# Exponentials of two units and of one in turn in six PSUM banks, and a burst of the other matmuls every three units

## The reference

```
c_kv = h @ W_dkv + b_dkv;  c_q = h @ W_dq + b_dq                      # width 128
k, v, q_base, q_rot from c_kv and c_q; k_rot = h @ W_kr; rotary on q_rot, k_rot
scores = einsum('bqhd,bkhd->bhqk', q, k) / sqrt(64)                   # 16 heads, 64 wide
out = softmax(scores) @ v
x = layernorm(h + out @ W_o + b_o)
x = layernorm(x + x @ int4_rounded(W_ffn) + b_ffn + (x @ a) @ b)
```

## Time and profile before

| | us |
|---|---|
| median of 3 runs | 2159.52 (2157.9 to 2245.24) |
| the profiled execution | 2158.53 |
| its slowest core's span (core 6) | 2157.0 |
| spans of the 8 cores | 2140.2 to 2157.0 |
| TensorE, ScalarE, VectorE busy | 1938.3, 2016.5, 602.7 |
| first and last start of an exponential | 121.2, 2088.5 |

### The profile page before, as it was taken

The page is one execution under the profiler, slowest core; times in us unless marked ns, Lnnn a source line. Parts: engine busy times, 40 slices in busy tenths (PEclk is TensorE's granted clock), DMA queues, the critical chain, the costliest instruction groups (busy, mean ns, idle before and its releaser), DMA issues.

```text
span 2157.0 us, 61016 instructions; the slowest of 8 cores (2140.2 to 2157.0 us)
## 1 busy us (share of the span) xinstructions
PE 1938.3 (90%) x22544; PEld 708.4 (33%) x22544; DVE 602.7 (28%) x1084; ACT 2016.5 (93%) x2177; POOL 256.6 (12%) x303
## 2 busy tenths in 40 slices
PE   5977888989999999998999999999999999999976
PEld 2422333333333333333333333333333333333323
DVE  2731411232223322222222322323222322322224
ACT  2689999989999999998999999999999999999973
POOL 2000000110011110110111100211111100211021
PEclk9999999999999999999999999999999999999998
DMA  9772300121122211221121211312121311323121
GB/s 166 164 148 80 107 23 27 51 92 43 36 83 67 87 45 53 71 71 69 41 93 50 99 36 36 103 54 81 45 92 48 102 31 41 102 85 118 41 70 39
DMA packets 78681, 155.69 MB, mean 72 GB/s; under 512 B 16192, under 2 KB 46912, under 8 KB 78400
## 3 DMA queue, kind: packets, MB, share of 16 engines
q1 hardware_dynamic: 64672, 106.86, 15.5%
q0 software_dynamic: 13728, 44.93, 8.7%
HBM read 109.75 MB, written 40.76 MB: 70 GB/s over the span
## 4 chain that ended last, share of the span: by engine, by line
ACT 69%; issue 16%; PE 6%; DMA 3%; DVE 2%; ACTq 2%; SPq 1%; POOL 0%; DVEq 0%; POOLq 0%
ACT Psb L1004 69%; ACTq L998 2%; DMA wbuf<-hG 1%; DMA rbc<-rec 1%; SPq L495 1%; PE PS L742 1%; PE PS L916 1%; PE PS L858 1%; PE PS L944 1%; DMA osb<-hG 1%; PE PS L729 1%; PE PS L879 1%; PE PS L774 1%; PE PS L769 1%; PE PS L754 1%
## 5 line engine op out<-in xcount | busy, mean ns | idle before, releaser
L1004 ACT ACTIVATE Psb<-PS 128x1024 bf16<-128x1024 f32 x2048 | 1933.9, 1025 | 34.8 <-PE PS L858 22.5
L858 PE MATMUL PS<-Qsb,Ksb 64*128 64x512 bf16 x4096 | 804.0, 387 | 149.4 <-ACT Psb L1004 138.5
L879 PE MATMUL PS<-Psb,Vsb 128*32 128x512 bf16 x8192 | 634.1, 386 | 0.5 <-ACT Psb L1004 0.5
L858 PEld LDWEIGHTS PS<-Qsb,Ksb 64*128 64x128 bf16 x4096 | 212.9, 93 | 702.5 <-issue 696.4
L889 PE MATMUL PS<-Psb,ones_sb 128*32 128x256 bf16 x8192 | 404.1, 274 | 3.5 <-issue 3.5
L889 PEld LDWEIGHTS PS<-Psb,ones_sb 128*32 128x32 bf16 x8192 | 221.7, 97 | 224.2 <-issue 8.1
L1154 DVE TENSOR_TENSOR X<-PS,X 128x512 f32<-128x512 f32 x112 | 77.5, 692 | 625.5 <-PE PS L835 330.0
L879 PEld LDWEIGHTS PS<-Psb,Vsb 128*32 128x32 bf16 x8192 | 127.9, 94 | 236.5 <-issue 236.5
L831 PE MATMUL PS<-wbuf,osb 128*128 128x512 bf16 x448 | 135.6, 384 | 0.0
L802 PE MATMUL PS<-wbuf,osb 128*128 128x512 bf16 x448 | 135.6, 384 | 0.0
L1126 DVE COPY rec<-PS 128x256 f32<-128x256 f32 x64 | 27.1, 423 | 344.9 <-PE PS L889 344.9
(11 more groups left out here) (111 smaller groups left out, 690.8 us busy)
## 6 DMA issues: line engine op xcount, KB each, us to landing
wbuf<-wo_p POOLq DMA_DIRECT2D x32, 512.0 KB, 7.0
rbc<-rec SPq DMA_DIRECT2D x512, 32.0 KB, 1.8
X<-h SPq DMA_DIRECT2D x28, 512.0 KB, 3.9
x_scr<-X SPq DMA_DIRECT2D x28, 512.0 KB, 2.6
X<-x_scr SPq DMA_DIRECT2D x28, 512.0 KB, 3.4
wbuf<-wf_p POOLq DMA_DIRECT2D x28, 512.0 KB, 6.9
out<-X SPq DMA_DIRECT2D x28, 512.0 KB, 2.6
X<-W_ffn SPq DMA_DIRECT2D x16, 512.0 KB, 4.4
```

The source lines that it names most:

```text
L858: m = pe.matmul(PS[:, b0 + 512 * hh:b0 + 512 * (hh + 1)], Ksb[rows, k0:k0 + 128], Qsb[rows, 512 * p:512 * (p + 1)], tile_position=(64 * hh ...
L879: pe.matmul(PS[32 * j:32 * (j + 1), b0:b0 + 512], Vsb[:, v0:v0 + 32], Psb[:, p0 + 512 * (j // 2):p0 + 512 * (j // 2 + 1)], start=first and ...
L1004: act.activation(Psb[:, 1024 * (g % 4):1024 * (g % 4 + 1)], PS[:, 1024 * (g % 2):1024 * (g % 2 + 1)], AF.Exp, scale=0.125).then_inc(sem["e ...
```

## The change

Three units now make one **period** (n in the code, 683 of them). Scores have six banks: the first two units of a period go to banks 0 to 3 and get one exponential of 2048 columns, the third goes to banks 4 and 5 and gets one of 1024. Values have bank 6 alone, and VectorE copies them to a new buffer xs at the end of a pair (pv_free lets the next pair's values in). Bank 7 is shared: in each period the side step writes it, VectorE empties it (side_out), the sums of the period write it, and VectorE adds them to rec (sums_in). On TensorE a period is: scores of the next period, then a burst of side step, values and sums. The o and f steps have 256 columns at 32-wide tiles, four at once, and each has half of the contraction, so there are 448 of them, each emptied by VectorE. One side step goes in a period; a planner (the while loop) gives 574 of the 683 periods one. The normalising steps are placed 1 to 5 periods after the pair's end: reciprocals 1, 2, 2, 3, DMAs 3, multiply 5. Exponential buffers in Psb are six units instead of four. The tail is the same but for the padded low-rank weights.

```diff
-    rec = sbt("rec", [128, 256], F32)
+    rec = sbt("rec", [128, 512], F32)
     rbc = sbt("rbc", [128, 512], F32)
+    xs = sbt("xs", [128, 512], F32)
...
+    NPER = (NG + 2) // 3
+    def per_units(n):
+        return range(3 * n, min(3 * n + 3, NG))
+    def parts(n):
+        us = per_units(n)
+        return [(P, [u for u in us if u // NKC == P])
+                for P in range(us[0] // NKC, us[-1] // NKC + 1)]
+    def end_of(P):
+        return ((P + 1) * NKC - 1) // 3
...
+    while main or qs:
+        whole = len(parts(n)) == 1
+        st = None
+        if qs and n >= want(qs[0]):
+            st = qs.pop(0)
+        elif main and n >= ready(main[0]) and (
+                whole or main[0][0] == "z" or main[0][1] == LAST - 1):
+            st = main.pop(0)
+        elif qs and n >= ready(qs[0]):
+            st = qs.pop(0)
+        if st:
+            when[st] = n
+            side[n] = st
+        n += 1
...
-        for k, off in enumerate((1, 2, 3, 4, 5, 5, 5 + max(1, NKC // 4 - 1))):
-            ep_at.setdefault(min((P + 1) * NKC + off, NG), []).append((P, k))
+        for k, off in enumerate((1, 2, 2, 3, 3, 5)):
+            ep_at.setdefault(min(end_of(P) + off, NPER), []).append((P, k))
...
+            def side_step(st, n):
+                qt, b0 = st[1], 3584
+                if n:
+                    pe.wait_ge(sem["den_free"], den_no[n - 1, parts(n - 1)[-1][0]] + 1)
...
+                if st[0] in ("o", "f"):
+                    sub, q, i = st[2:]
+                    f = st[0] == "f"
...
+                        w0 = 1024 * c + 256 * q
+                        for j in range(4):
+                            m = pe.matmul(PS[32 * j:32 * (j + 1), b0:b0 + 256],
+                                          osb_tok(qt, sub, c)[:, 32 * j:32 * (j + 1)],
+                                          wbuf[:, w0:w0 + 256], start=(c == 4 * i),
+                                          stop=(c == 4 * i + 3 and not (f and i)))
+                    if f and i:
+                        for j in range(4):
+                            m = pe.matmul(PS[32 * j:32 * (j + 1), b0:b0 + 256],
+                                          zb_sb[:, 32 * j:32 * (j + 1)],
+                                          bpad_sb[:, 256 * q:256 * (q + 1)], start=False, stop=True)
...
-                b0 = 1024 * (g % 2)
+                b0 = 1024 * (g % 3)
...
                     pe.wait_ge(ld_krot[kc // 4 % 2], 32 * (kc // 8 + 1))
-                if g >= 2:
-                    pe.wait_ge(sem["exp_done"], g - 1)
+                if g >= 3 and g % 3 != 1:
+                    pe.wait_ge(sem["exp_done"], g - 1 if g % 3 == 0 else g - 2)
...
+            def values(P, us):
+                p = P % NP
+                for u in us:
+                    if u == P * NKC:
+                        if P:
+                            pe.wait_ge(sem["pv_free"], P)
+                        else:
+                            pe.wait_ge(sem["ev_v"], 8 * NSP)
+                    p0 = 1024 * (u % 6)
                     for j in range(4):
                         v0 = 1024 * (u % NKC) + 128 * p + 32 * j
-                        pe.matmul(PS[32 * j:32 * (j + 1), b0:b0 + 512], Vsb[:, v0:v0 + 32],
-                                  Psb[:, p0 + 512 * (j // 2):p0 + 512 * (j // 2 + 1)],
-                                  start=first and u == g, stop=last and u > g)
-                if g == 0:
+                        m = pe.matmul(PS[32 * j:32 * (j + 1), 3072:3584], Vsb[:, v0:v0 + 32],
+                                      Psb[:, p0 + 512 * (j // 2):p0 + 512 * (j // 2 + 1)],
+                                      start=(u % NKC == 0), stop=(u % NKC == NKC - 1))
+                if us[-1] % NKC == NKC - 1:
+                    m.then_inc(sem["pv_end"], 1)
+            def sums(n, P, us):
+                if n == 0:
                     pe.wait_ge(sem["init"], 4)
-                if first and P:
-                    pe.wait_ge(sem["den_free"], P)
-                for u in (g, g + 1):
+                if den_no[n, P]:
+                    pe.wait_ge(sem["den_free"], den_no[n, P])
+                pe.wait_ge(sem["ev_misc"], misc_by[n])
+                for u in us:
                     for j in range(4):
-                        p0 = 1024 * (u % 4) + 256 * j
-                        m = pe.matmul(PS[32 * j:32 * (j + 1), 3072:3328], ones_sb[:, :],
-                                      Psb[:, p0:p0 + 256], start=first and u == g,
-                                      stop=last and u > g)
-                m.then_inc(sem["pv_done"], 2)
-            for g in range(NG):
-                scores(g)
-                if g % 2 and g >= 3:
-                    values(g - 3)
-                for st in bg_at.get(g, ()):
-                    if st[0] in ("qr", "qp"):
-                        q_step(st)
-                    else:
-                        tail_step(st)
-            values(NG - 2)
+                        p0 = 1024 * (u % 6) + 256 * j
+                        m = pe.matmul(PS[32 * j:32 * (j + 1), 3584:3840], ones_sb[:, :],
+                                      Psb[:, p0:p0 + 256], start=(u == us[0]), stop=(u == us[-1]))
+                m.then_inc(sem["den_done"], 1)
+            def burst(n):
+                pe.wait_ge(sem["exp_done"], per_units(n)[-1] + 1)
+                if n in side:
+                    side_step(side[n], n)
+                for P, us in parts(n):
+                    values(P, us)
+                    sums(n, P, us)
+            for u in per_units(0):
+                scores(u)
+            for n in range(NPER):
+                if n + 1 < NPER:
+                    for u in per_units(n + 1):
+                        scores(u)
+                burst(n)
             pe.wait_ge(sem["exp_done"], NG)
...
-                    act.wait_ge(sem["ev_v"], 8 * NSP)
-                act.activation(Psb[:, 1024 * (g % 4):1024 * (g % 4 + 1)],
-                               PS[:, 1024 * (g % 2):1024 * (g % 2 + 1)],
-                               AF.Exp, scale=0.125).then_inc(sem["exp_done"], 1)
+                if n == 1:
+                    act.wait_ge(sem["st_rqa"], 16)
+                    act.wait_ge(sem["st_rqc"], 16)
+                act.wait_ge(sem["s_done"], us[1] + 1)
+                p0 = 1024 * (us[0] % 6)
+                act.activation(Psb[:, p0:p0 + 2048], PS[:, 0:2048], AF.Exp, scale=0.125
+                               ).then_inc(sem["exp_done"], 2)
+                if len(us) == 3:
+                    if n == 0:
+                        act.wait_ge(sem["ev_v"], 8 * NSP)
+                    act.wait_ge(sem["s_done"], us[2] + 1)
+                    p0 = 1024 * (us[2] % 6)
...
+            def sums_in(n, P, us):
+                d = den_no[n, P]
+                acc, src = rec[:, 256 * (P % 2):256 * (P % 2 + 1)], PS[:, 3584:3840]
+                dve.wait_ge(sem["den_done"], d + 1)
+                if us[0] == P * NKC:
+                    if P >= 2:
+                        dve.wait_ge(sem["ld_rec"], 128 * (P - 1))
+                    if P == 0:
+                        dve.wait_ge(st_rk[1], 32 * (NSP // 2))
+                    dve.tensor_copy(acc, src).then_inc(sem["den_free"], 1)
+                else:
+                    dve.wait_ge(sem["den_free"], d)
+                    dve.tensor_tensor(acc, src, acc, op=ALU.add).then_inc(sem["den_free"], 1)
...
+            def values_out(P):
+                dve.wait_ge(sem["pv_end"], P + 1)
+                if P:
+                    dve.wait_ge(sem["nrm_done"], P)
+                else:
+                    dve.wait_ge(sem["rope_q"], 5)
+                dve.tensor_copy(xs[:, :], bank(6)).then_inc(sem["pv_free"], 1)
...
+                        dve.wait_ge(sem["mm_misc"], misc_no["f", qt - 2, 3, 3, 1] + 1)
+                    if p >= 3 and qt < LAST:
+                        if p == 4:
+                            dve.wait_ge(sem["st_rqc"], 16 * (qt + 2))
+                        elif p == 5:
+                            dve.wait_ge(sem["st_rqa"], 16 * (qt + 2))
+                        else:
+                            dve.wait_ge(sem["rope_q"], 5 * (qt + 2))
+                    dve.wait_ge(sem["pv_free"], P + 1)
+                    dve.tensor_tensor(osb_pair(qt, p), xs[:, :], rbc[:, :], op=ALU.mult
                                       ).then_inc(sem["nrm_done"], 1)
...
+                if st[0] == "z":
+                    dve.tensor_copy(zb_sb[:, :], PS[:, 3584:3712]).then_inc(sem["ev_misc"], 1)
+                if st[0] in ("o", "f"):
+                    sub, q, i = st[2:]
+                    n = ln_no(qt, 1 if st[0] == "o" else 2, sub)
+                    dve.wait_ge(sem["bias_in"], n + 1)
+                    dve.wait_ge(sem["ev_misc"], m)
+                    dve.tensor_tensor(Xq(n, q), PS[:, 3584:3840], Xq(n, q), op=ALU.add).then_inc(sem["ev_misc"], 1)
+                    if i and q % 2:
...
+            for n in range(NPER + 1):
+                if n < NPER:
```

(7 more changed lines are left out.)

488 lines of the change are left out of this document (231 added, 257 removed).

## The result

The changed kernel takes **2358.36 us** (median of 4 runs, 2356.32 to 2360.54), the kernel before beside it 2159.52 us: a ratio of 1.0918, 95% interval 1.0897 to 1.0939. In some executions of any kernel the cores of one die show a lower clock and take longer (one of the four of the kernel before took 2245.24 us); times and ratios in this document leave out those over 1% longer, and of the kernel "side step first", whose profiled execution has it mildly on cores 4 to 7, the periods are those of cores 0 to 3. The change is slower by 9%, inside the range and at its upper end: the profiled executions are 200 us apart (2358.62 against 2158.53), 143 were forecast.

A forecast was written before the change was run, and what follows sets the result against it. ScalarE's exponentials bound the kernel before, with TensorE close behind; VectorE's emptying would join the pacing loop. Terms 22+6-8+52+43+7+12+7+2 = +143 on 2158.5 gave 2300 us, range 2195 to 2360.

The forecast's parts named there:

- The loop (+22): Middle-tile periods with a side step: sums wait for VectorE to empty bank 7, 2.89 us against 2.853, +22 us.
- the first tile's +7: First tile: 85 periods at 2.75 instead of 2.79 us, plus six pair ends at 1.6 us, +7 us together.
- The multiply (+52): Normalising multiply five periods after a pair's end: VectorE waits for rec copies, delaying the next evacuation; 47 x 1.1, +52 us.
- Pair ends (+43): Periods where a pair ends: evacuation, xs copy and old sums delay the new pair's sums and scores; 36 x 1.2, +43 us.
- Double exponentials: ScalarE's 2048-column exponential: lasts 1.89 us at 0.87 per further 1024 columns; 1.86 to 1.92 would confirm the slope.
- The removed instruction: ScalarE: each of 683 removed exponentials saves 0.03 us, 20 us in all, only where it doesn't wait for scores.
- the clock: Rival: TensorE's granted clock falls to 0.97, each TensorE term longer, +30 us on the forecast, 2330 us; chance 0.10, mostly this.
- The rival in which VectorE's loop does not bind: Side step's sums start within 1.10 us, so the 2.75 loop or ScalarE's 2.67 holds: 2100 us; chance 0.09.
- A: The double exponential of a period on ScalarE, taken to last 1.89 us.
- The one in which its blocks do not bind: Rival: VectorE's loop binds, but copies land in time or pair ends fall into slack: 2190 us, about same; chance 0.17.

The follow-up runs named there:

- side step first: The changed kernel with the side step moved ahead of the third unit's scores and the wait for the period's exponentials: 2336.72 us, ratio 1.0796 to the kernel before.
- the short copy: The changed kernel with VectorE copying only 64 of the 512 values columns to xs at a pair's end: 2359.92 us, ratio 1.0922 to the kernel before.
- the run with two singles: The changed kernel with each double exponential split in two, each releasing its own scores: 2362.09 us, ratio 1.0890 to the kernel before.

## Why the prediction held, and where its sizes were off

**The loop (+22)** was right in kind and link by link, 0.08 long in 3; its size was small, since o and f periods away from the blocks have a mean of 2.97 where the loop had 2.89. It is told by the 443 waits, by the periods of the side step that fell when VectorE's emptying was cut, and by 2.79 when TensorE's order was turned. Periods without a side step have a median of 2.73, forecast 2.75. With +143 forecast and 149 us measured in periods at full clock, the sum of these terms stood, and not only by errors that cancel. By kind of period, over the 2.85 of before: end+6 with a side step 58 us (forecast 52), pair ends 40 (43), all others 54 (48). Inside the others two things do cancel: the first tile's +7 came out as nothing (2.82 us a period in both kernels), and the periods of the 28 transposing steps, for which the working has no term, measure 3.25, +10.

**The multiply (+52)** was the largest term and right in mechanism: right place (the burst at end+6), waits for rbc in every case, though of 2.3 us in 64 places and not of about 1 in 50. Taking it out is worth 69 us by ratio: (3.85 - 2.93) x 55 = 51 at its place, as forecast, of which other periods take 9 back ((3.070 - 3.008) x 682 = 42 in all at full clock), and 20 less in low-clock periods, for which the term had no place.

**Pair ends (+43)**: 3.93 against about 3.0 of the other periods of this kernel, 0.93 x 36 = 33 by the count of the forecast, which had 1.2 x 36 = 43. The working put xs on the path between the emptying and the old pair's sums; the short copy shows that the three uses of bank 7 alone give the same 3.9.

**Double exponentials**: 1.877 us, forecast 1.86 to 1.92. Slope from 1.018 for 1024: 0.859 for 1024 more, 0.16 fixed. The removed instruction was put at 0.03 us, from two-pointer rows; the run with two singles gives 1.96 - 1.88 = 0.08. The Trainium skill (ScalarE: Activation LUTs, What ACT_TABLE_LOAD costs) gives 186 ns and 0.833 ns a column, of which 93 ns overlap back to back; by that rule, an estimate, 1024 columns take 1.04 us, 2048 columns 1.89 and an instruction more costs 0.09, and the trace agrees within 0.01 to 0.02 us. It still changed nothing, as ScalarE does not set this pace.

**The missed terms.** First, the weights' maximum: its wait for two DMAs had 20.0 us in the trace of before, on VectorE, and I did not ask what the change queues behind it. About +15. Second, the clock: as a rival it had a chance of 0.10 and +30 on top of the forecast, 2330, and 0.97 at some 80% busy; measured are 0.97 at 82% and some +30 in low-clock periods beside the stall, so the forecast's mechanism and this rival came together, and 2358 lies nearer to 2330 than to 2300. These two are 45 of the 57 us between the terms' sum and the measured loss; 6 more are in the full-clock periods and 4 in the later start. That the result still lies inside the range, 2 us below its upper end, is in part luck: that end was made of the clock, 15 us at the multiplies and 50 us for a slower double exponential, which did not come, and nothing in it stood for the stall of the weights' maximum. The rival in which VectorE's loop does not bind fell: 139.9 us of waits for X. (The remark there that the page's slope makes A 0.014 us shorter should say 0.017, 0.870 less 1024 x 0.833 ns; nothing hangs on it.) The one in which its blocks do not bind fell with the multiply's 70 us.
